# Image 1's second down projection ahead of image 0's last, VectorE's low parts reordered, and TensorE's wait for its own matmuls taken out

## What is computed

```python
x = x + _L0_attn_ref(_layernorm(x), w_attn, b_attn, w_proj, b_proj)
# _L0_ffn_ref, on _layernorm(x):
gate = jax.nn.silu(jnp.einsum('bsh,ih->bsi', x, w_gate))
up = jnp.einsum('bsh,ih->bsi', x, w_up)
x = x + jnp.einsum('bsi,hi->bsh', gate * up, w_down)
```

## Time and profile before

| what | us |
|---|---|
| median of three runs | 840.65 (839.3 to 842.49) |
| the profiled execution, its own time | 835.43 |
| its span, first to last instruction | 833.7 |
| PE busy | 783.2 (94%) |
| DVE busy | 645.4 (77%) |
| POOL busy | 296.9 (36%) |

### The profile page before, as it was taken

One profiled execution on the slowest core, in us unless ns is written; L12 is line 12 of the kernel. 1 busy time (PEld: TensorE's weight loads), 2 busy tenths in 40 slices (PEclk: granted clock), 3 DMA queues, 4 the chain that ended last, 5 costly groups with the idle time before them and its releaser, 6 DMA issues.

```text
span 833.7 us, 13393 instructions
## 1 busy us (share of the span) xinstructions
PE 783.2 (94%) x4554; PEld 542.9 (65%) x4554; DVE 645.4 (77%) x1609; ACT 417.5 (50%) x796; POOL 296.9 (36%) x436
## 2 busy tenths in 40 slices
PE   3999899999999999999998999999999999999998
PEld 2755465556555565556554577888877778888886
DVE  6598787887988778877887256759999687888773
ACT  4336666665666555666567424333436334334341
POOL 6223234342433424424334404323450033443342
PEclk9999999999999999999999999999999999999999
DMA  8873556565666475736662425042115421121052
GB/s 284 209 251 123 175 184 205 166 181 177 200 210 192 131 220 180 248 105 212 215 190 89 173 83 184 26 151 73 42 50 177 140 98 72 71 76 51 14 166 99
DMA packets 75372, 122.80 MB, mean 147 GB/s; under 512 B 13075, under 2 KB 38342, under 8 KB 75305
## 3 DMA queue, kind: packets, MB, share of 16 engines
q1 hardware_dynamic: 74217, 121.69, 45.7%
q10 hardware_dynamic: 1088, 0.26, 0.1%
HBM read 79.34 MB, written 42.32 MB: 146 GB/s over the span
## 4 chain that ended last, share of the span: by engine, by line
PE 56%; DVE 20%; DMA 10%; ACT 4%; issue 4%; SPq 3%; POOL 2%; ACTq 0%; DVEq 0%
PE bank L1280 19%; PE bank L1916 10%; PE bank L1199 6%; PE bank L1111 5%; PE bank L1126 5%; PE bank L1182 4%; PE bank L1158 4%; DVE bank L919 4%; DMA pv_dram<-weighed 3%; DMA weighed<-pv_dram 2%; PE bank L1115 2%; ACT pt L751 2%; SPq L500 1%; DVE stats L176 1%; DMA row_sums<-pv_dram 1%
## 5 line engine op out<-in xcount | busy, mean ns | idle before, releaser
L751 ACT ACTIVATE pt<-bank 128x512 f32<-128x512 f32 (+1 forms) x384 | 196.7, 530 | 124.7 <-PE bank L1182 122.4
L919 DVE CUSTOM_DVE_ANT_0 bank<-bank,mask_qk 128x512 f32<-128x512 f32 (+3 forms) x416 | 195.8, 511 | 42.2 <-PE bank L1158 40.9
L1182 PE MATMUL bank<-q_st,k_st 116*128 116x512 bf16 (+3 forms) x512 | 132.1, 301 | 12.2 <-ACT pt L751 11.4
L1158 PE MATMUL bank<-k_st,q_st 97*128 97x512 bf16 (+3 forms) x512 | 132.1, 304 | 8.0 <-DMA q_st<-slopes_dram 4.2
L1511 POOL TENSOR_TENSOR wd_lo<-wd_raw,wd_hi 128x512 fp32r<-128x512 f32 x33 | 43.5, 1323 | 162.8 <-ACT wd_hi L1541 162.8
L656 POOL TENSOR_SCALAR_AFFINE_SELECT pt<-pt 128x256 f32<-128x256 f32 x128 | 56.5, 441 | 118.9 <-ACT pt L751 118.9
L1158 PEld LDWEIGHTS bank<-k_st,q_st 97*128 97x128 bf16 x512 | 41.8, 98 | 70.8 <-issue 36.5
L660 POOL TENSOR_SCALAR_AFFINE_SELECT pt<-pt 128x256 f32<-128x256 f32 x128 | 54.2, 424 | 78.3 <-ACT pt L751 78.0
L1199 PE MATMUL bank<-pt,v_nat 128*32 128x512 f32 (+3 forms) x1024 | 77.2, 443 | 3.0 <-POOL pt L656 2.3
L1916 PE MATMUL bank<-wd_hi,w_hi 128*128 128x512 f32 x176 | 70.1, 398 | 4.8 <-DVE wd_lo L1693 2.0
L1182 PEld LDWEIGHTS bank<-q_st,k_st 116*128 116x128 bf16 x512 | 45.8, 98 | 43.0 <-ACT pt L751 20.7
(11 more groups left out here) (186 smaller groups left out, 1713.6 us busy)
## 6 DMA issues: line engine op xcount, KB each, us to landing
stack_dram<-scratch SPq DMA_DIRECT2D x32, 384.0 KB, 3.1
q_st<-stack_dram SPq DMA_DIRECT2D x32, 384.0 KB
k_st<-stack_dram SPq DMA_DIRECT2D x32, 384.0 KB
wd_raw<-w_down SPq DMA_DIRECT2D x44, 256.0 KB, 3.6
xt<-w_gate_up SPq DMA_DIRECT2D x20, 512.0 KB, 3.6
stack_dram<-scratch SPq DMA_DIRECT2D x32, 256.0 KB, 3.4
pv_dram<-weighed SPq DMA_DIRECT2D x32, 256.0 KB, 4.3
weighed<-pv_dram SPq DMA_DIRECT2D x17, 256.0 KB
```

What stands on the lines that cost most here:

```text
L751: act.activation(pt[:, h % PT_RING, COL0[k]:COL0[k] + WIDE[k]], bank[3 + (3 * h + k) % 2][:, 0:WIDE[k]], ACT.Exp, scale=1.0 / HD).then_inc ...
L919: last = dve.tensor_tensor_reduce(bank[k][:, at:at + n], bank[k][:, at:at + n], mask_qk[:, S - n:S], 1.0, NEG, ALU.add, ALU.max, mx[:, h % ...
L1158: last = pe.matmul(bank[k][:, at:at + n], q_st[0:K_MAX, s, h % 4, t * P:(t + 1) * P], k_st[0:K_MAX, s, h % 4, 0:n], start=True, stop=not b ...
L1182: last = pe.matmul(bank[3 + u % 2][:, at:at + n], k_st[0:K_EXP, s, h % 4, t * P:(t + 1) * P], q_st[0:K_EXP, s, h % 4, t * P:S], start=True ...
```

## The change

`DOWNS` is written in another order: down 10 is (1, 0), down 11 is (1, 1), down 12 is (0, 10), downs 13 to 21 are (1, 2) to (1, 10), and the same in the second pair. `END` grows by one. Around it:
- TensorE runs three whole downs ahead of the loop at a pair's end, and nine in it. T0 and T1 stand after downs 13 and 15.
- ScalarE casts the products of downs 10 and 11 and the weights of down 12 ahead of unit 5's second Silu (and so in unit 16).
- GpSimd makes `wd_lo` of down 11 in unit 5; VectorE made it before.
- VectorE makes `gu_lo` of downs 10 and 11 directly after its sixth sum. In unit 5 `weight_sums_lo` moves behind `gu_lo` of down 12, and `down_lo(12)` stands between `gu_even` and that.
- `down_done` counts only downs with inner tiles 0 to 9; TensorE's wait for `sum_done` and its own count are gone. ScalarE's two waits go through the new `downs_over`, which picks `sum_done` or `down_done`.
- SP's list has the same loads and stores in the same places; what load 11 and load 12 fetch is exchanged.

```diff
-    DOWNS = [(0, f) for f in range(FT - 1)] + [(1, 0), (0, FT - 1)] + [(1, f) for f in range(1, FT)]
+    DOWNS = [(0, f) for f in range(FT - 1)] + [(1, 0), (1, 1), (0, FT - 1)] + [(1, f) for f in range(2, FT)]
...
-    END = {FIRST - 1: FT, len(UNITS) - 1: PAIR + FT}
+    END = {FIRST - 1: FT + 1, len(UNITS) - 1: PAIR + FT + 1}
...
+        def downs_over(eng, count):
+
+            if count > 0:
+                b, f = DOWNS[count - 1]
+                if f == FT - 1:
+                    eng.wait_ge(sum_done, (b + 1) * TT)
+                else:
+                    eng.wait_ge(down_done, sum(g < FT - 1 for _, g in DOWNS[:count]))
...
+                if u == FIRST - 1:
+                    down_lo(END[u] - 1)
...
-                need(act, down_done, n - WD + 1)
+                downs_over(act, n - WD + 1)
...
-                need(act, down_done, n - GU + 1)
+                downs_over(act, n - GU + 1)
...
                 if u in END:
+                    down_hi(END[u] - 1)
+                    product_hi(END[u] - 2)
+                    product_hi(END[u] - 1)
                     down_hi(END[u])
-                    product_hi(END[u] - 1)
...
-                weight_sums_lo(u + 1)
+                if u != FIRST - 1:
+                    weight_sums_lo(u + 1)
                 if u in END:
+                    product_lo(END[u] - 2)
                     product_lo(END[u] - 1)
...
+                if u == FIRST - 1:
+                    down_lo(END[u])
                 product_lo(DOWNS.index((2 * pair, f)))
                 if u == FIRST - 1:
-                    down_lo(FT)
+                    weight_sums_lo(u + 1)
                 if u in END:
-                    for i in range(FT - 1):
+                    for i in range(FT - 2):
...
                 if f == FT - 1:
                     last.then_inc(sum_done, 1)
-                    if t == TT - 1:
-                        pe.wait_ge(sum_done, (b + 1) * TT)
-                        pe.sem_inc(down_done, 1)
...
                 if u in END:
+                    whole_down(END[u] - 2)
                     whole_down(END[u] - 1)
                     whole_down(END[u])
-                    for i in range(FT - 1):
+                    for i in range(FT - 2):
```

More of the change, by code:

```diff
@@ L1475, in _ @@
                     n, b = END[u], UNITS[u][0] * 2
-                    for i in range(n + 1, n + 6):
+                    for i in range(n, n + 5):
                         load_down(i)
                     store(b)
-                    for i in range(n + 6, n + 9):
+                    for i in range(n + 5, n + 8):
                         load_down(i)
                     load_residual(b + 1)
-                    for i in range(n + 9, n + FT + 2):
+                    for i in range(n + 8, n + FT + 1):
                         load_down(i)
@@ L1532, in _ @@
                 if u == len(UNITS) - 1:
-                    for n in range(END[u], END[u] + FT):
+                    for n in range(END[u] - 1, END[u] + FT):
                         down_lo(n)
@@ L1688, in down_lo @@
             def down_lo(n):
-                if n == FT:
-                    dve.wait_ge(wd_lo_done, FT)
+                if n == END[FIRST - 1]:
+                    dve.wait_ge(wd_lo_done, n)
                 dve.wait_ge(wd_hi_done, n + 1)
```

## The result

The changed kernel takes 833.48 us (median of 18 runs), the kernel before, run in turn with it, 838.11 us (18 runs). The ratio is 0.9944 (95% interval 0.9926 to 0.9961), so it is 0.56% faster. Three of the changed kernel's 18 runs took 885.67, 979.21 and 2734.11 us and are left out of the ratio (as is a run of 1989.12 us from that of the best of the first pair); the median of the other 15 is 833.33. Forecast was 835.9 us, from 840.65, which is a ratio of 0.9944.

What follows compares the result with a forecast made beforehand. TensorE, busy 94% of the span, was taken as the bound, so only gaps between its matmuls could give: 0.56 + 2.32 + 0.56 + 0.82 + 0.56, less 0.1, 4.7 us off 840.65: 835.9. Case range 834.0 to 838.0; 8-in-10 range 834.0 to 838.7.

Steps and rivals of the forecast that it cites:

- The anchor: The level the forecast started from: the shown median of 840.65 us, from which the gain of 4.7 was taken.
- The bounds: The forecast case's limits: gain 4.0 to 5.2 us, with 1.5 us for the runs' spread, giving 834.0 to 838.0.
- Gap 1: TensorE's stop ahead of down 10, waiting for its low part behind the weight sums: gain 0.56 us.
- the sentence on down 11's `wd_lo` at GpSimd: In unit 5, it follows down 10's at 616.58, takes 1.3 to 1.5 us, and is there by 618.1, for 623.51.
- Gap 2: TensorE's stop ahead of image 0's last down, to be covered wholly by two downs: gain 2.32 us.
- Gaps 3 to 5: TensorE's waits for itself behind downs 11, 21 and 33: gains of 0.56, 0.82 and 0.56 us.
- The drain-only rival: Behind downs 11, 21 and 33, removing self-waits gives only 0.5 us; whole gain 3.4, 837.3 us; chance 0.11.
- The 0.1 taken off for the five waits of unit 6: At unit 6's start, three waits beyond two may keep 0 to 0.26 us of the gain away; 0.1 assumed.
- The walk through the rest of the pair: From down 12 to unit 6: T1's and down 19's stops stay, unit 6 starts at 658.14, 4.16 us earlier.
- The VectorE rival: Slowed VectorE subtractions run into T0's chain, delaying T1 and down 19: gain 2.5 to 3.9, about 837.5 us; chance 0.12.
- Load 39: Rival: image 2's later stores delay this load, stopping TensorE at down 39; 842 us if landing takes 13; chance 0.04.
- The sum: Gains at five TensorE gaps, 0.56 + 2.32 + 0.56 + 0.82 + 0.56 = 4.82 us, less 0.1: 4.7.

Runs made afterwards that it cites:

- the best of the first pair: Changed kernel with GpSimd's second wd_lo subtraction later and low parts of downs 19 and 20 ahead of combination subtractions: feed-forward 204.19 us, ratio 0.9915 to the kernel before.

## Why the prediction was right or wrong

- **The anchor was wrong, and with it the range.** The prediction noted that the median shown lay 5.2 above the profiled execution, "put down to the runs", and took 4.7 from 840.65. The bounds gave the level 1.5 us, although the profiled execution, which the prediction had in hand, lay 5.2 away. (By its own terms the upper bound is 838.15, not 838.0.) The kernel before had 838.11 as its median over 18 runs, and 836.22 and 839.04 over 29 and 17 in the experiments. So three runs fixed the level to no better than 2 to 4 us, and this step failed: the level was taken from them as if it were known to 1.5. The same ratio on 838.11 is 833.4. The range should have carried that uncertainty beside those of the terms. The trace had a sign of it, the 0.98 in the last part of the attention.
- **Gap 1 was wrong: 0.56 forecast, 0.09 had** (620.56 to down 10's last start 623.84 is 3.28, after 620.82 to 624.01, 3.19). The step that failed is the sentence on down 11's `wd_lo` at GpSimd. It asked whether that would be ready and not what it would hold up. It runs from 616.8 to 618.5, just over VectorE's next subtraction, which took 1.52 us in place of 0.41. The run with it moved gave 0.51 back.
- **Gap 2 was right: 2.32.** From down 10's last start to down 11's is 2.72 now and was 5.04. The slack was smaller than worked out, since `gu_even` and its low part slipped by the same 1.1: `gu_lo` at 625.3 in place of 624.0, for 626.96.
- **Gaps 3 to 5 were right in size**, 0.56, 0.8 and 0.57, and by their own run 2.04 in all. The drain-only rival falls. The prediction's explanation, a semaphore's trip and the restart, was incomplete: the wait brings back only 1.10 of 1.95, restarts included, and the count behind it the other 0.85. No run tells a semaphore's trip from the drain. The 0.1 taken off for the five waits of unit 6 was not needed; there the step is 0.22.
- **The Trainium skill's price for the waits**, three drains of 166 ns, an estimated 0.5 us by its page "TensorE: Matmul & The Clock Gate" (section "Single matmul latency"), is too low for this pattern: the rows decide for 2.0. The wait alone, at 1.10 for the three, is also twice that.
- **The walk through the rest of the pair was right.** T1's idle is 0.51, VectorE's low part of the 19th down is there 10.34 us after L1745 begins, as before, and that down stops as its predecessor did. The VectorE rival falls: the residual additions ended at 630.6, T0 did not wait.
- **Load 39** was issued at about 803.0, which is 806.5 on the clock of the rows before (down 32 now starts 3.47 earlier) where the rival had 806.9. Its cast began at 805.93, 6.7 us ahead of down 39 (793.58 + 7 x 2.72 = 812.6). Nothing stopped there, so this rival falls too.
- **The sum**: 0.09 + 2.32 + 0.56 + 0.79 + 0.57 = 4.33, and 4.30 measured.

## What to carry to other kernels

Before work is handed to a second engine, read what the first engine does in the same microsecond: the price can be a stall of a neighbour that is neither moved nor waited for. A wait of TensorE for its own matmuls cost 0.37 us a place here and a count behind it 0.28 more, though the same count is free in a running stream: so test both together, in their place. Compare small edits by a stretch of the trace that repeats to 0.1 us, and hang the forecast of an absolute time on more than three runs, with their spread in the range.

## What the runs showed of the hardware

- A 128x256 subtraction on VectorE took 1.52 us beside GpSimd's subtraction and 0.41 without it, with the same operands.
- TensorE's wait for its own last matmul costs 0.22 us plus 0.11 of slower starts behind it. A semaphore counted up by TensorE itself costs nothing in a full stream and lengthens the gap by 0.24 us behind such a wait, by 0.51 where unit 6's first matmul follows.
- The granted clock drops to half for 3.5 us at a time (seldom 7.0) in the attention part, from never to four times in one execution of identical code, and the feed-forward starts some 2 us later with each on average. TensorE had been partly idle ahead of each drop, but the same idleness also passed without one.
